# Grouping the transpositions of the attention probabilities by query tile, with the value product in the order of the groups

## What is computed

```python
k = x @ W_lat + b_lat
q = (x @ W_d + b_d).reshape(Bx, Tx, NH, L)
q = jnp.transpose(q, (0, 2, 1, 3))
att = jnp.einsum('bhtl,bsl->bhts', q, k) * scale
att = jnp.where(causal[None, None], att, -jnp.inf)
att = jax.nn.softmax(att, axis=-1)
y = jnp.einsum('bhts,bsl->bhtl', att, k)
y = jnp.transpose(y, (0, 2, 1, 3)).reshape(Bx, Tx, NH * L)
return y @ W_proj + b_proj
```

## Time and profile before

| what | value |
|---|---|
| median of 3 runs | 320.69 us (320.29 to 321.52) |
| span of the profiled execution, first to last instruction | 319.7 us |
| mean granted TensorE clock | 0.986 |
| PE busy | 293.6 us, 1962 matmuls |
| DVE busy | 252.6 us |
| ACT busy | 212.1 us |
| POOL busy | 150.7 us |

### The profile page before, as it was taken

How to read it: one execution, slowest core, us unless ns; L and a number is a source line. 1 busy time by engine, 2 the same in 40 slices (tenths; PEclk the granted TensorE clock), 3 DMA queues, 4 the chain that set the end, 5 groups by cost and what they waited for, 6 DMA issues and landing times.

```text
span 319.7 us, 6333 instructions
## 1 busy us (share of the span) xinstructions
PE 293.6 (92%) x1962; PEld 264.0 (83%) x1962; DVE 252.6 (79%) x698; ACT 212.1 (66%) x585; POOL 150.7 (47%) x202
## 2 busy tenths in 40 slices
PE   8987999999999999999997899899699999985991
PEld 4766999999999998898896798788589999875991
DVE  2688887888778888888888888877978886688484
ACT  2686777777777776777674677686457778541532
POOL 4695444443333555555548555079553221473011
PEclk9999999999999999999999999999799999998998
DMA  6591111111111111111102101011100000000013
GB/s 189 99 321 36 34 36 33 37 45 33 33 37 44 33 33 35 33 37 33 33 2 66 36 25 30 13 33 37 33 16 18 18 2 0 3 0 2 0 33 100
DMA packets 17739, 13.44 MB, mean 42 GB/s; under 512 B 1433, under 2 KB 17458, under 8 KB 17714
## 3 DMA queue, kind: packets, MB, share of 16 engines
q1 hardware_dynamic: 17714, 13.13, 14.0%
HBM read 12.07 MB, written 1.05 MB: 41 GB/s over the span
## 4 chain that ended last, share of the span: by engine, by line
PE 76%; DVE 11%; issue 5%; ACT 5%; SPq 1%; DMA 1%; POOLq 0%; DVEq 0%; ACTq 0%
PE bank L358 14%; PE bank L360 14%; PE bank L359 14%; PE bank L457 10%; PE ps_out L358 5%; PE ps_out L359 5%; PE ps_out L360 5%; PE bank L507 2%; PE bank L437 2%; DVE probs L891 1%; ACT probs L714 1%; DVE beats L1050 1%; DVE probs L941 1%; DVE ties L1055 1%; ACT pT_hi L721 1%
## 5 line engine op out<-in xcount | busy, mean ns | idle before, releaser
L714 ACT ACTIVATE probs<-probs,negmax 128x512 f32<-128x512 f32 (+3 forms) x128 | 72.5, 574 | 10.2 <-DVE negmax L891 8.7
L721 ACT CAST pT_hi<-bank 128x512 fp32r<-128x512 f32 (+2 forms) x96 | 43.6, 488 | 45.8 <-PE bank L457 45.8
L1158 POOL TENSOR_TENSOR wd_hi<-wd_raw,zero 128x256 fp32r<-128x256 f32 x32 | 23.7, 740 | 86.2 <-PE bank L360 79.7
L891 DVE CUSTOM_DVE_ANT_0 probs<-bank,mask_row 128x512 f32<-128x512 f32 (+3 forms) x128 | 58.9, 480 | 0.6 <-PE bank L360 0.6
L898 DVE TENSOR_TENSOR pT_lo<-bank,pT_hi 128x512 fp32r<-128x512 f32 (+2 forms) x96 | 52.8, 551 | 7.4 <-ACT pT_hi L721 7.2
L457 PE MATMUL bank<-ident,probs 128*128 128x128 f32 x320 | 46.4, 276 | 11.4 <-issue 11.0
L457 PEld LDWEIGHTS bank<-ident,probs 128*128 128x128 f32 x320 | 37.8, 141 | 20.2 <-issue 14.2
L941 DVE TENSOR_SCALAR probs<-probs,rinv 128x384 f32<-128x384 f32 (+2 forms) x96 | 51.4, 589 | 0.8
L358 PE MATMUL ps_out<-wp_hi,yT_hi 128*128 128x256 f32 x128 | 38.6, 302 | 0.1
L358 PE MATMUL bank<-kT_hi,qT_hi 128*128 128x512 f32 (+2 forms) x96 | 37.8, 394 | 0.2 <-DVE qT_lo L845 0.2
L360 PE MATMUL ps_out<-wp_hi,yT_lo 128*128 128x256 f32 x128 | 36.1, 282 | 0.0
(11 more groups left out here) (146 smaller groups left out, 769.4 us busy)
## 6 DMA issues: line engine op xcount, KB each, us to landing
wd_raw<-in_L_attn_W_d SPq DMA_DIRECT2D x32, 128.0 KB, 2.2
wp_raw<-in_L_attn_W_proj SPq DMA_DIRECT2D x32, 128.0 KB, 2.1
wf_raw<-in_L_ffn_w SPq DMA_DIRECT2D x2, 1024.0 KB, 6.4
x_nat<-in_L_attn_x SPq DMA_DIRECT2D x4, 256.0 KB, 2.9
out<-x SPq DMA_DIRECT2D x3, 256.0 KB, 3.1
out<-x SPq DMA_DIRECT2D x2, 128.0 KB, 1.9
wlat_raw<-in_L_attn_W_lat SPq DMA_DIRECT2D x1, 128.0 KB, 3.5
bproj_all<-in_L_attn_b_proj SPq DMA_DIRECT2D x1, 128.0 KB, 3.6
```

The source lines that it names most:

```text
L714: act.activation(p_tile(s, j), p_tile(s, j), ACT.Exp, bias=negmax[:, s, j:j + 1], scale=-1.0, accum_out=sums[:, s, j:j + 1]).then_inc(exp_ ...
L721: act.copy(pT_hi[:, turns[n][3]], turns[n][2]).then_inc(pt_hi_done, 1)
L891: dve.tensor_tensor_reduce(p_tile(s, j), score_bank[j], mask_row[:, (TILES - 1 - j) * P:], -SCALE, -MASKED, ALU.add, ALU.min, accum_out=ne ...
L1158: pool.tensor_tensor(hi, src, nothing, ALU.add).then_inc(hi_done, 1)
```

## The change

The ten transpositions are grouped by query tile. Turn 0 is now query tile 3: squares (3,0), (3,2), (3,1) and (3,3), the last of them `pT_last`. Turn 1 is query tile 2, three squares. Turn 2 is query tiles 1 and 0, three squares. Each turn's split is 384 columns. The squares lie in slots of `pT_hi` and `pT_lo`, numbered so that every turn writes, and every product reads, slots at an equal step.

```diff
-PT_OFF = {2: 0, 1: 2 * P, 0: 5 * P}
-PT_COLS = 9 * P
+PT_SLOT = {0: range(2, 10, 2), 1: range(0, 15, 5), 2: range(7, 11, 2)}
+PT_COLS = 11 * P
...
+        turns = [([(3, 0), (3, 2), (3, 1), (3, 3)], ps_t0, 8, 1),
+                 ([(2, 1), (2, 0), (2, 2)], ps_t1, 5, 1),
+                 ([(1, 1), (0, 0), (1, 0)], ps_t0, 0, 2)]
...
                 if n == 0:
                     wait(pe, norm_act, p)
+                    wait(pe, pt_last_done, p - 1)
+                elif n == 1:
+                    wait(pe, norm_dve, p * 3 - 2)
+                else:
                     wait(pe, norm_dve, p * 3)
+                    wait(pe, pt_last_done, p)
...
+                wait(pe, pt_lo_done, p * 3 - 1)
+                keys(2, 2, 4, first=True)
                 wait(pe, pt_last_done, p)
-                pe.matmul(ps_y[:, SEQ - P:], k_last[b][:, :], pT_last[:, :], start=False, stop=True).then_inc(y_ready, 1)
+                pe.matmul(ps_y[:, SEQ - P:], k_last[b][:, :], pT_last[:, :], start=False, stop=False,
+                          skip_group_check=True)
+                keys(0, 2, 4)
+                wait(pe, pt_lo_done, p * 3)
+                keys(1, 1, 4)
+                keys(0, 0, 2, last=True).then_inc(y_ready, 1)
```

More of the change, by code:

```diff
@@ L453, in turn @@
                     pe.wait_ge(x_split, CH + n + 1)
-                a = 0
-                for i in tiles:
-                    for j in range(i, TILES):
-                        last = pe.transpose(dst[:, a:a + P], p_tile(s, j)[:, i * P:(i + 1) * P], ident[:, :])
-                        a += P
+                for a, (j, i) in enumerate(tiles):
+                    last = pe.transpose(dst[:, a * P:(a + 1) * P], p_tile(s, j)[:, i * P:(i + 1) * P], ident[:, :])
                 last.then_inc(pt_ready, 1)
@@ L926, in period @@
                     k_low(0)
+                if at.live(-1):
+                    turned(at, 2)
                 if at.live(1) and at.fixed >= 0:
@@ L936, in period, with normalise @@
                     dve.reciprocal(rinv[:, s, :], sums[:, s, :]).then_inc(rinv_done, 1)
+                    wait(dve, rinv_done, p + 1)
+                    normalise(at, (2,))
                 late_piece(at)
                 if at.live(0):
[L939 to L942 removed]
+                    normalise(at, (1, 0))
+            def normalise(at, js):
+                s = at.place(0)
+                for j in js:
+                    dve.tensor_scalar(p_tile(s, j), p_tile(s, j), rinv[:, s, j:j + 1], None,
+                                      ALU.mult).then_inc(norm_dve, 1)
             def early_piece(at):
```

43 lines of the change are left out of this document (21 added, 22 removed).

## The result

| | median, us | range | span of the profiled execution, us |
|---|---|---|---|
| before | 320.49 | 318.75 to 321.52 | 319.7 |
| changed | 324.21 | 323.11 to 325.75 | 321.7 |

The changed kernel is slower: the ratio is 1.0138, with an interval of 1.0087 to 1.019. The forecast of 320.4, its range of 317.8 to 323.3 and its sign were wrong. The profiled execution of the changed kernel took 323.44 us, 1.7 more than its span. The median difference is 3.7 us, and these two profiled executions show 2.0 of it. All four profiles are used from here on.

A forecast was written before the change was run, and what follows sets the result against it. PE alone was taken to set the loop's pace, with ten waits at turn 0 outside it; -0.03 - 0.85 + 0.33 - 0.7 + 0.3 + 0.69 = -0.26 us gave 320.4 us from 320.69, range 317.8 to 323.3.

The forecast's parts named there:

- The wait moves and does not go: PE's wait at turn 0 moves to the queries, its end by 0.03 us; of 9.0 us, 0.03 gained.
- In periods without an early piece nothing is gained: 0: DVE and ACT loop without an early router piece: normalisation at D + 5.79 against D + 5.78, D being `yT_lo`'s start.
- What spreads it: DVE normalisations take far longer while POOL works; 0.1 us shifts become 0 or 0.8; +-1 us over about ten periods.
- The early pieces, -0.85: DVE and ACT loop in periods 18, 20, 21, 23, 24: chain 0.17 us shorter each, -0.85 us.
- Periods 27 and 28, +0.05: Behind the longest wait, where PE was slow: exponentials later by the same reckoning as period 25, +0.05 us.
- Rival 2: Longest wait changes: PE's clock stays up or DVE's last normalisation precedes POOL's 1.94 us; 318.9 us, chance 0.18.
- The start, -0.7: First two turns: without `yT_lo` in period 1 queries start 0.63 us earlier; with the second turn, -0.7 us.
- The value product, +0.3: One 512-column product becomes two of 256: 0.02 us a unit in 16 periods, +0.3 us.
- The end, +0.69: Periods 31 and 32, no scores covering turn 2's split: +0.27 and +0.42, +0.69 us, between +0.3 and +1.0.
- The offset of 1.0 us between span and median: Whole kernel: median taken 1.0 us above the profiled span, 320.69 against 319.7 before, 320.4 against 319.4 after.
- Rival 1: The waits go: queries do not hold PE, 10.1 us less, -0.26 - 9.0, some 311 us; chance 0.05.
- Rival 3: Turn 2 holds the queries on ACT and DVE: ten periods at 0.28, +2.8 us, 323.2; chance 0.15.

The follow-up runs named there:

- All four profiles: Kernel before and changed kernel, each unchanged and profiled twice: spans 319.7 and 317.8 us before, 321.7 and 322.5 us changed.
- The memset on POOL: Changed kernel plus a one-column memset on POOL between the two halves of the `wp` split: 321.81 us, ratio 1.0054.
- the four kernels with another order on DVE: Changed kernel with turn 2's step behind the queries (320.07 us), tile 3's maxima ahead of `yT_lo` (317.28), both (317.41), or those maxima plus one 512-column product (317.11).
- the maxima first: Changed kernel with DVE's maxima of tile 3 ahead of `yT_lo`, a one-column memset carrying the wait: 317.28 us, ratio 0.9906.
- a second one: Kernel before with DVE's maxima of tile 3 ahead of `yT_lo`, nothing of the change: 319.77 us, ratio 1.0006.

## Why the prediction was wrong, point by point

- **The wait moves and does not go: right.** It went from turn 0 to the queries, released by `negmax`, 0.23 us behind the last instruction of the maxima (127.25 to 127.48), as computed. That its end moves by only 0.03 us was right in kind; put back, the wait costs 0.3 to 1.6 us in all, not clear of the noise.
- **"In periods without an early piece nothing is gained: 0": this is the step that failed.** The chain up to the normalisation was right (5.75 us against 5.79). The step then took the length of the normalisations as unchanged, and it is not a constant of the kernel: 1.85 or 2.46 us, by which engine wins. Before, the race was lost in one of the six periods 13 to 18 in one profile (15) and in none in the other; after, in all six. Five or six periods by 0.6 are 3.0 or 3.6, less the 0.6 that the change gains in period 18 (8.18 to 7.64 where the race is won): 2.4 to 3.0, and the table shows 2.24 and 2.90. The memset on POOL, which undoes the loss alone, takes 3.5 us out of this stretch.
- **"What spreads it", +-1 us, named the cause and mis-sized it.** It says that normalisations are far longer while POOL works and that shifts of 0.1 us can become 0 or 0.8. It took +-1 us for ten periods, which fits shifts that average out. They do not in the changed kernel: each of periods 13 to 18 has the same work as the last, the distance between the two engines repeats to 0.02 us, and so does the loss. The rows to see it were at hand: the two kinds of period of the kernel before, 0.01 us apart.
- **The early pieces, -0.85: the mechanism right, the gain given back.** In period 21 `yT_lo` to the normalisation took 6.08 us; in the changed kernel it takes 5.88 (176.13 to 182.01), 0.20 less for the 0.17 computed. But DVE's normalisation of tile 2 now stands ahead of the late piece and starts 0.22 us behind the reciprocal, whose result it needs, where the late piece started 0.10 behind it. That it is held to 0.85 us is not new: in the kernel before the first normalisation of this period took 0.87. Changed kernel, then the kernel before:

```profile
181.79 0.18 DVE L957 RECIPROCAL rinv<-sums 128x4 f32<-128x4 f32 x1 [0.25 <-ACT probs L735]
182.01 0.85 DVE L967 TENSOR_SCALAR probs<-probs,rinv 128x384 f32<-128x384 f32 x1
182.78 0.95 DVE L1060 SCALAR_TENSOR_TENSOR sel<-x,rw_all 128x256 fp32r<-128x256 f32 x1
...
185.00 0.68 DVE L927 TENSOR_TENSOR yT_lo<-bank,yT_hi 128x512 fp32r<-128x512 f32 x1
...
180.76 0.18 DVE L936 RECIPROCAL rinv<-sums 128x4 f32<-128x4 f32 x1 [0.36 <-ACT probs L714]
180.86 0.89 DVE L1034 SCALAR_TENSOR_TENSOR sel<-x,rw_all 128x256 fp32r<-128x256 f32 x1
...
183.82 0.68 DVE L906 TENSOR_TENSOR yT_lo<-bank,yT_hi 128x512 fp32r<-128x512 f32 x1
```

  From ACT's normalisation to the next `yT_lo` it is 2.99 us (182.01 to 185.00), and it was 2.84 (180.98 to 183.82). Of 0.20 gained, 0.15 is lost. From period 19 to 26 the two pairs show -0.11 and +0.18 for the -0.4 that the steps give there (-0.68 for four of the five periods, +0.28 for period 25).
- **Periods 27 and 28, +0.05: right in sum.** Together +0.23 and +0.12: period 27 is shorter by 0.7 to 1.0 and period 28 longer by 1.0 to 1.1. The longest wait stayed (2.7 us), and so did PE's lower level behind it: granted 0.84, with 0.83 in the earlier trace rows. Rival 2 did not happen in this kernel's two profiles; in those of the four kernels with another order on DVE the clock stayed up and the two periods were 1.7 to 2.8 us shorter, with a shorter wait in it. At the same wait of 2.7 us, in the kernel before, the full clock was worth 1.2 to 1.3, near the 1.4 that it was given.
- **The start, -0.7: right on average** (-1.58 and +0.14); its scatter of 0.8 to 0.95 us within one kernel comes for the larger part (0.60 and 0.64 us) from how long POOL's splits hold the normalisations of period 2.
- **The value product, +0.3: 0.4.** The loop's periods grew by 0.04, not 0.02; 0.01 to 0.03 of it is the split of the product (7.547 to 7.521 us, and 7.527 to 7.513 with the maxima first), and the rest stays open.
- **The end, +0.69: 0.8 and 1.0** from period 28 on. The wait for the third split stands at the last two value products as described.
- **The offset of 1.0 us between span and median** was wrong: in the result the run's time is 1.7 us above the span, and the first profile of before was near the upper end of its range. It does not enter the difference.
- **The rivals.** Rival 1's "10.1 us less" does not fit its own sum (0.26 + 9.0 are 9.3); it plays no part in the result. Rival 3 gave a time nearest to the one measured, 323.2, but by another mechanism (a later normalisation); the normalisation is not later. A rival by the right one was missing: "POOL wins in every period from 13 to 18", five more than in the profile at 0.6 each, would have put 3.0 on top of 320.4, 323.4.

Taken together for the first pair: -1.58 at the start, +0.38 in the loop, +2.24 in periods 13 to 19, -0.11 up to 26, +0.23 in 27 and 28, +0.8 at the end: +2.0. For the second: +0.14, +0.38, +2.90, +0.18, +0.12, +1.0: +4.7. The medians, 3.7 to 4.4 apart, lie between.

## What to carry to other kernels

Where an instruction of one engine has two lengths in a trace, find out what decides between them before its mean is put into a sum; in a periodic program the answer can be the same in every period. Removing a wait from an engine helps by no more than the next wait leaves, so the next wait is moved out of the way in the same step: here one edit alone made the kernel 1.4% slower, a second one alone did nothing, and both together made it 0.9% faster. When a few hundredths of a microsecond decide, a dummy instruction on one engine can show it, if the same one, put where that engine waits anyway, changes nothing.

## What the runs showed of the hardware

A normalisation on DVE (`TENSOR_SCALAR`, 128x384, fp32, SBUF to SBUF) took 0.42 us when it started first by 0.05 us or more, and 0.85 to 1.00 when POOL's `TENSOR_TENSOR` of 128x256 had started up to 0.11 us before it or up to 0.03 us behind it in the records; POOL's took 0.73 to 0.75 when it won, 0.95 to 0.97 when it came 0.05 or 0.06 us behind, and 0.83 when it came 0.18 behind. At 0.04 us both outcomes stand in one execution. Behind waits of 2.7 to 2.8 us in period 27, PE's granted clock over the next five microseconds was 0.66 to 0.70 in nine profiles and 1.00 in one; behind nine waits of 2.1 to 2.4 us it was 1.00, but for one with 0.66. That a shift of 0.04 us on an engine that is busy for 46% of the span moves the whole kernel by 2.4 us was not expected. A memset of one column on POOL took 0.09 us and moved the instruction behind it by only 0.04.
